# Attention product over whole rows with block-diagonal weights, in a fused attention and feed-forward layer

## The reference, cut to what matters

```python
q = layernorm(silu(causal_dwconv(h @ Wq, ...)))     # per head, 128 features
k = layernorm(silu(causal_dwconv(h @ Wk, ...)))
v = h @ Wv
beta = sigmoid(h @ Wb + bb);  gate = silu(h @ Wg)
def step(S, inp):                                   # over the 64 tokens
    q_t, k_t, v_t, b_t = inp
    S = (1.0 - b) * S + b * (v_t[..., :, None] * k_t[..., None, :])
    return S, einsum('bhvk,bhk->bhv', S, q_t)
x = x + (o * gate) @ Wo
# adapters, in the second part
xa = einsum('btd,brd->btr', x, A[idx]);  delta = einsum('btr,bor->bto', xa, Bm[idx]) * s[idx]
```

## Time and profile before

| | us |
|---|---|
| median of the 3 runs shown | 2570.62 (2568.57 to 2571.15) |
| the profiled execution | 2573.15 |
| its span, first to last instruction | 2571.4 |
| PE busy | 2450.2 (95%) |
| DVE busy | 1633.6 (64%) |
| ACT busy | 1072.2 (42%) |
| POOL busy | 783.9 (30%) |
| mean granted TensorE clock | 0.979 |

### The profile page before, as it was taken

The page is one execution under the profiler, slowest core; times in us unless marked ns, Lnnn a source line. Parts: engine busy times, 40 slices in busy tenths (PEclk is TensorE's granted clock), DMA queues, the critical chain, the costliest instruction groups (busy, mean ns, idle before and its releaser), DMA issues. The chain is left out here.

```text
span 2571.4 us, 38384 instructions
## 1 busy us (share of the span) xinstructions
PE 2450.2 (95%) x14292; PEld 1849.9 (72%) x14292; DVE 1633.6 (64%) x2653; ACT 1072.2 (42%) x1615; POOL 783.9 (30%) x636
## 2 busy tenths in 40 slices
PE   7789899999999999999999999999999999999976
PEld 5567677777777777777777777777777777777754
DVE  4666456676667756576566766667666775657653
ACT  4554444444435334443434434444443533444321
POOL 3465433322323222232233232232132322223230
PEclk9899999999999999999999999999999999999987
DMA  7786766567665776666676676656757577666750
GB/s 233 255 309 220 258 224 231 194 204 258 201 222 185 238 232 199 207 202 226 212 231 196 201 249 212 222 187 219 253 192 228 186 231 233 205 203 203 228 173 17
DMA packets 326962, 551.38 MB, mean 214 GB/s; under 512 B 98354, under 2 KB 122970, under 8 KB 326778
## 3 DMA queue, kind: packets, MB, share of 16 engines
q1 hardware_dynamic: 315778, 529.75, 62.2%
q10 hardware_dynamic: 11000, 19.18, 2.3%
HBM read 495.08 MB, written 53.74 MB: 213 GB/s over the span
## 5 line engine op out<-in xcount | busy, mean ns | idle before, releaser
L526 POOL TENSOR_TENSOR og_lo<-gt,og_hi 128x512 fp32r<-128x512 f32 x128 | 181.6, 1418 | 1128.3 <-ACT og_hi L1040 1128.3
L1110 PE MATMUL pj_a<-ht_hi,wq 128*128 128x512 f32 x1024 | 361.3, 414 | 30.8 <-ACT gt L1033 21.3
L1110 PE MATMUL pj_a<-ht_hi,wg 128*128 128x512 f32 x1024 | 355.5, 408 | 17.2 <-DMA wg<-parts_g 12.9
L812 DVE SCALAR_TENSOR_TENSOR y_q<-pj_a,conv,y_q 128x504 f32<-128x504 f32 (+2 forms) x384 | 281.1, 732 | 137.9 <-ACT y_q L1016 128.7
L1110 PE MATMUL pj_b<-ht_hi,wk 128*128 128x512 f32 x1024 | 346.7, 399 | 8.4 <-DMA wk<-parts_k 8.3
L1110 PE MATMUL ring<-wo,og_hi 128*128 128x512 f32 x1024 | 324.3, 398 | 5.2 <-issue 5.2
L1110 PE MATMUL ring<-wv,ht_hi 128*128 128x512 f32 x1024 | 320.5, 394 | 4.5 <-POOL wv L516 4.5
L812 DVE SCALAR_TENSOR_TENSOR y_k<-pj_b,conv,y_k 128x504 f32<-128x504 f32 (+2 forms) x384 | 281.4, 733 | 56.0 <-ACT y_k L1016 46.8
L522 POOL TENSOR_TENSOR y_k<-y_k,sq_k 128x512 f32<-128x512 f32 x128 | 170.8, 1335 | 462.2 <-DMA sq_k<-m_rows 462.1
L1110 PEld LDWEIGHTS pj_b<-ht_hi,wk 128*128 128x128 f32 x1024 | 192.4, 188 | 107.1 <-issue 52.0
L1110 PEld LDWEIGHTS pj_a<-ht_hi,wq 128*128 128x128 f32 x1024 | 197.6, 193 | 80.2 <-issue 24.9
(11 more groups left out here) (202 smaller groups left out, 4645.6 us busy)
## 6 DMA issues: line engine op xcount, KB each, us to landing
wq<-parts_q SPq DMA_DIRECT2D x112, 512.0 KB, 4.2
wk<-parts_k SPq DMA_DIRECT2D x112, 512.0 KB, 6.2
wg<-parts_g SPq DMA_DIRECT2D x112, 512.0 KB, 5.9
wv<-parts_v SPq DMA_DIRECT2D x112, 512.0 KB, 6.5
wo<-parts_o SPq DMA_DIRECT2D x112, 512.0 KB, 6.7
sq_q<-m_rows SPq DMA_DIRECT2D x110, 256.0 KB, 3.8
sq_k<-m_rows SPq DMA_DIRECT2D x110, 256.0 KB, 4.5
sq_q<-r_rows SPq DMA_DIRECT2D x110, 256.0 KB, 3.5
```

The source lines that it names most:

```text
L526: G.tensor_tensor(og_lo[:, u % OG_RING, :], gt[:, u % GT_RING, :], og_hi[:, u % OG_RING, :].bitcast(F32), ALU.subtract).then_inc(S["oglo"], 1)
L812: V.scalar_tensor_tensor(out=yy[:, :, k:], in0=pp[:, :, :L - k], scalar=conv[:, i, h, 3 - k:4 - k], in1=yy[:, :, k:], op0=ALU.mult, op1=AL ...
L1110: last = T.matmul(psum, a, b, start=start and n == 0 and m == 0, stop=stop and n == len(pairs) - 1 and m == 2)
```

## The change

1. **The product with v.** A new tile `decay_bd` of 128 x 512 is zeroed once by GpSimd. `weigh` writes the weighed scores of even sequences to its upper 64 rows and of odd ones to its lower 64 rows, each at its own 64 columns, in two instructions of 64 partitions x 256. Every 128 columns then hold two diagonal blocks and zeros beside them. `attend` makes four products, each with 128 rows of v as weights and 128 columns of `decay_bd`, all in the ring's bank; m0 is no longer written by it.
2. **The gate.** `gate_out` is one instruction of 128 x 512. The semaphore `og_odd` is gone: `score` and `scan` of the next unit wait for `weighed` instead of for the gate and the product; `weigh` waits for the preceding unit's product.
3. **The adapter product** is scaled in place in its PSUM bank, which is released after the low part is made; `xam` and two semaphores are gone, `gamma_cols` moves to `acc`, and `load_x(1)` also waits until it was sent off.

```diff
 def adapt(g, i):
-    V.tensor_tensor(rows8(xam[:]), rows8(ring_bank("xa", g, i)[:, 0:HALF]), sc.broadcast_to([P, HROWS, L]),
-                    ALU.mult).then_inc(taken_sem("xa", g, i), 1)
-    dve.wait_ge(*taken("xa", g, i))
+    down = ring_bank("xa", g, i)[:, 0:HALF]
+    V.tensor_tensor(rows8(down), rows8(down), sc.broadcast_to([P, HROWS, L]), ALU.mult).then_inc(S["xam_mul"], 1)
+    dve.wait_ge(S["xam_mul"], 2 * g + i + 1)
...
 def scan(u):
     if u:
-        dve.wait_ge(*made("pv", u - 1))
+        dve.wait_ge(S["weighed"], 2 * u)
...
 def weigh(u):
     dve.wait_ge(S["scores"], u + 1)
     dve.wait_ge(S["scanned"], u + 1)
-    V.tensor_tensor(decay[:], m0[:, 0:HALF], decay[:], ALU.mult).then_inc(S["weighed"], 1)
+    if u:
+        dve.wait_ge(*made("pv", u - 1))
+    else:
+        dve.wait_ge(S["setup_pool"], 9)
+    for b in range(2):
+        half = slice(b * L, (b + 1) * L)
+        V.tensor_tensor(even_odd(decay_bd[half, :], b), m0[half, 0:HALF].rearrange("p (i t) -> p i t", t=L),
+                        decay[half, :].rearrange("p (i t) -> p i t", t=L), ALU.mult).then_inc(S["weighed"], 1)
...
 def gate_out(u):
-    for b, bank_ in enumerate((ring_bank("pv", u, 0), m0)):
-        th = even_odd(t, b)
-        V.tensor_tensor(th, bank_[:, 0:HALF].rearrange("p (i t) -> p i t", t=L), th, ALU.mult
-                        ).then_inc((taken_sem("pv", u), S["og_odd"])[b], 1)
+    V.tensor_tensor(t, ring_bank("pv", u, 0)[:], t, ALU.mult).then_inc(taken_sem("pv", u), 1)
...
 def score(u):
     if u:
-        pe.wait_ge(S["og_odd"], u)
+        pe.wait_ge(S["weighed"], 2 * u)
...
 def attend(u):
-    pe.wait_ge(S["weighed"], u + 1)
+    pe.wait_ge(S["weighed"], 2 * u + 2)
...
-    for b in range(ROWS):
-        at, cols = L * (b % 2), slice(b // 2 * L, (b // 2 + 1) * L)
-        mm = T.matmul((ring_bank("pv", u, 0), m0)[b % 2][:, cols], v[at:at + L, s % 2, b // 2, j * P:(j + 1) * P],
-                      decay[at:at + L, cols], start=True, stop=True)
+    for i in range(HT):
+        cols = slice(i * P, (i + 1) * P)
+        mm = T.matmul(ring_bank("pv", u, 0)[:, cols], v[:, s % 2, i, j * P:(j + 1) * P], decay_bd[:, cols],
+                      start=True, stop=True)
```

More of the change, by code:

```diff
@@ L137, in adaln_attn_ffn @@
         decay = sb("decay", [P, HALF])
+        decay_bd = sb("decay_bd", [P, GROUP])
         gt = sb("gt", [P, GT_RING, GROUP])
@@ L149, in adaln_attn_ffn @@
         b_hi, b_lo = sb("b_hi", [P, D], F32R), sb("b_lo", [P, D], F32R)
-        xam = sb("xam", [P, HALF])
         xam_hi, xam_lo = sb("xam_hi", [P, HALF], F32R), sb("xam_lo", [P, HALF], F32R)
@@ L179, in adaln_attn_ffn @@
         conv_rows, small_rows = gt[0:H, 0:2, :], gt[0:H, 2, :]
-        gamma_cols = xam[0:KC, 0:P]
+        gamma_cols = acc[0:KC, 1, 0, 0:P]
         TAB_LOADS, LATE_LOADS = 4 + 4 + 1, 1 + 1 + 2
@@ L191, in adaln_attn_ffn @@
             sq_q sq_k seed newton_a newton_b rr n_q n_k aff_q aff_k
-            scanned og_odd oghi oglo ht_hi beta_done keep_done x2_hi xam_mul xam_hi xam_lo ssq absmax small
+            scanned oghi oglo ht_hi beta_done keep_done x2_hi xam_mul xam_hi ssq absmax small
             row_seed qa qb quant biased scaled""".split()
@@ L304, in load_x @@
                     sp.wait_ge(*made("sw", 0, KC - 1))
+                    sp.wait_ge(S["gamma_out"], 16)
                 elif g > 1:
@@ L509, in _ @@
                                pattern=[[RANK, NAD]], channel_multiplier=-1).then_inc(S["setup_pool"], 1)
+            pool.memset(decay_bd[:], 0.0).then_inc(S["setup_pool"], 1)
             def split_lo(block_):
@@ L700, in adapt @@
                 sc = ad_scale[:, b0:b0 + HROWS].rearrange("p (b o) -> p b o", o=1)
-                V.tensor_tensor(rows8(xam[:]), rows8(ring_bank("xa", g, i)[:, 0:HALF]), sc.broadcast_to([P, HROWS, L]),
-                                ALU.mult).then_inc(taken_sem("xa", g, i), 1)
-                dve.wait_ge(*taken("xa", g, i))
+                down = ring_bank("xa", g, i)[:, 0:HALF]
+                V.tensor_tensor(rows8(down), rows8(down), sc.broadcast_to([P, HROWS, L]), ALU.mult).then_inc(S["xam_mul"], 1)
+                dve.wait_ge(S["xam_mul"], 2 * g + i + 1)
                 if i:
                     dve.wait_ge(*made("h", g, 1))
-                V.tensor_copy(xam_hi[:], xam[:]).then_inc(S["xam_hi"], 1)
+                V.tensor_copy(xam_hi[:], down).then_inc(S["xam_hi"], 1)
                 dve.wait_ge(S["xam_hi"], 2 * g + i + 1)
-                V.tensor_tensor(xam_lo[:], xam[:], xam_hi[:].bitcast(F32), ALU.subtract).then_inc(S["xam_lo"], 1)
+                V.tensor_tensor(xam_lo[:], down, xam_hi[:].bitcast(F32), ALU.subtract).then_inc(taken_sem("xa", g, i), 1)
             def row_scales(g, p):
@@ L1036, in gated_hi @@
                 act.wait_ge(*taken("pv", u))
-                act.wait_ge(S["og_odd"], u + 1)
                 if u >= OG_RING:
@@ L1195, in dense @@
                         pe.wait_ge(S["wo_in"], wo_loads("h", g))
-                pe.wait_ge(S["xam_lo"], 2 * g + t // 2 + 1)
+                pe.wait_ge(*taken("xa", g, t // 2))
                 free_bank("h", g, t)
```

## The result

The changed kernel takes 2559.68 us (median of 9 runs, 2550.77 to 2563.38); the kernel before, timed on the same chip between them, 2571.92 (9 runs, 2568.57 to 2578.60). The ratio is 0.9949 [0.9936, 0.9962]; it is estimated from the single runs and is not quite the quotient of the two medians (0.9952). By the medians the change saves 12.2 us, where 28.2 were forecast. The profiled execution took 2562.26.

A forecast was written before the change was run, and what follows sets the result against it. TensorE's stream was taken as the bound between 410 and 2490 us. 37.1 + 1.0 - 2.4 - 4.1 - 2.0 - 0.7 - 0.7 = 28.2 us saved, from 2573.15 to 2544.9 profiled, 2542.4 as median; range 2532 to 2557.

The forecast's parts named there:

- The attend step: TensorE, last 512-column product to third q product: 1.93 us becomes 1.59, saving 0.34 per unit, mostly border gaps.
- How often it counts: The 0.34 us counts in 109 attend steps, units 15 to 123: 37.1 us; the 15 units before add 1 us.
- (a): Slot 10, g projection's wait for wg: one attend step's 0.34 us is lost in 7 groups, 2.4 us.
- where it is given back: Step listing recurring TensorE waits, ended by something started earlier, that absorb savings: 2.4, 4.1 and 2.0, plus 0.7 us.
- (b): Slot 15, k projection's wait for wk: two attend steps, 0.68 us, are lost in 6 groups, 4.1 us.
- (c): Slot 0, q projection's wait for ht_lo: slot 15's attend step, 0.34 us, is lost in 6 groups, 2.0 us.
- (d): Slot 12, gate read ahead of q: about 0.1 us late in 7 groups, 0.7 us.
- VectorE: Split weighing and merged gate: +0.27 us per unit, +0.45 without overlap; only slot 10 pays, 0.7 us taken.
- B: VectorE and the loads fall behind in slots 8 to 10 and 13 to 15: 14 us left, 2556; chance 0.10.
- D: Lengthened waits in slots 10 and 15 make the clock fall, 3.3 us each; with all 13, 2585; chance 0.03.
- C: The absorbing waits move with TensorE and the first part gains too: 42 us saved, 2528.5; chance 0.05.
- E: Whole-row weight loads on TensorE don't hide: +0.55 us per unit, 60 in 109, 2630 us; chance 0.02.

The follow-up runs named there:

- e13: The changed kernel run again without further edits, on one chip with later runs: 2555.47 us, ratio 0.9941 to the kernel before.
- e9: The changed kernel with the eight cond loads issued in slot 10 instead of slot 13: 2544.88 us, ratio 0.9883.
- e10: The kernel before with the eight cond loads issued in slot 10 instead of slot 13: 2565.82 us, ratio 0.9970.
- e11: The changed kernel with cond loads in slot 10 and the head's own loads ahead of those of Wv, Wo and W2: 2530.24 us, ratio 0.9833.
- e12: The kernel before with cond loads in slot 10 and the head's own loads ahead of those of Wv, Wo and W2: 2561.58 us, 0.9958.
- e2: The kernel before with only its weighing split into two instructions of 64 rows: 2576.01 us, ratio 1.0015.
- e3: The changed kernel with one weighing of 128 x 256 instead of two, block-diagonal layout left out (result not the reference's): 2554.7 us, ratio 0.9928.
- e16: The changed kernel with the product with v as eight of 64 columns over whole rows instead of four of 128: 2628.86 us, ratio 1.0214.
- e4: The changed kernel with five added 512-column products ahead of the waits in slots 15 (wk) and 10 (wg), groups 1 to 7: 2550.87 us, 0.9928.
- e14: The changed kernel with five added 512-column products ahead of the waits in slots 15 and 10, a repetition: 2551.44 us, ratio 0.9925.

## Why the prediction was wrong

**The attend step: right.** 1.59 us by the sum, 1.59 measured, in each of its three parts. The border gaps are gone, as argued. Whole slots shorten by 0.36, 0.02 more than I used.

**How often it counts: right but for slot 0.** That slot shortens by 0.13 instead of 0.36 in groups 2 to 6 and is 0.37 longer in group 1 (1.8 us given back in six groups). Its attend step follows four float32 transposes of 16 x 16 and not 512-column products. The gap ahead of the step is 0.14 in both kernels, and afterwards its second half starts 0.22 behind the first, where it is 0.11 elsewhere. I had read one border and used it for all; in slot 9, behind bf16 transposes, 0.27 is saved.

**(a) Slot 10: the mechanism right, the size low.** Forecast 2.4 for wg and 0.7 for VectorE in seven groups; 4.3 in six were measured in the profiled pair and 6.9 with the trace of e13. The gap for wg grew by 2.5 and 3.6, that for the weighing by 0.6 and nothing; one fall of the clock lies there in the first trace (2047.9) and three in the other, for which the sum had nothing.

**The step that failed: "where it is given back".** The sum let the wait for wk in slot 15 take 4.1 us, at full clock, and put the clock and every other load at nothing. (b), the wait itself: its anchor was right, its length was not fixed. The gap grew by 7.3 us in the profiled pair and by 3.4 with the trace of e13, so its size is met within what one execution scatters. With the cond loads elsewhere (e9, e10) the slot is 23.7 us in both kernels, and the difference between them goes from 14.2 to 20.9.

**The clock: put at nothing.** "The granted clock stays 1.00 between 410 and 2450 us" was wrong. Four falls lie in slots 10 and 15 of groups 1 to 6 in each of the two traces of the changed kernel, and none in that of the kernel before. By the mean clocks of all runs this is worth 5 us, and the added products took 4 to 8 us back.

**Other loads: put at nothing.** I named three waits and took the rest as covered. Slots 5 and 7 gave back 6.8 us, 5.7 with the trace of e13. Of the 6.8, 5.1 is the growth of their gaps ahead of the k projection (1.8 to 5.0 and 1.4 to 3.3), at loads that stand behind those of Wv, Wo and W2; with e13 it is 3.8. The busy share of 95% had hidden that these loads arrive with a few tenths to spare. With both edits (e11, e12), where no load ends these waits, the change is worth 31.3 us. That this is near 28.2 is partly luck. Without the terms for wg and wk the sum would be 28.2 + 2.4 + 4.1 = 34.7; in their place the waits for VectorE in slot 10 became longer than forecast (6.8 given back there in six groups).

**(c) and (d): right.** The wait in slot 0's q projection takes up the attend step of slot 15 (0.42 in the earlier trace rows; the gap there went from 0.69 to 0.84 although its border is gone). Slot 12 loses 0.13 a group, 0.1 forecast.

**VectorE: the mechanism named, the size too low.** +0.51 per unit instead of +0.27, above the bound of +0.45, for which 0.7 us was put in the sum. e2 and e3 give 1 to 5. Ahead of the attend steps of the other slots in groups 1 to 6 the weighing still ends 1 us or more early, as was said. Of the 3.7 us by which TensorE's wait for it grows in e2, 1.5 lie in slot 10 (four times), 0.9 in the first part and 1.4 in the tail; the 0.7 of the sum were for slot 10 alone.

**The rivals.** B was what happened in kind (14 us left by its count, 12.2 measured), but by the loads and the clock more than by VectorE, and with a chance of 0.10. That its number is so near is luck, since it has no term for the clock. D came in part: I wanted 9 of 13 waits to fall and priced one at 3.3 us. There were four in the one trace and five in the other, mostly of 3.4 us at half clock, which is 1.7 us each. What I held against it, that no wait of the steady part is longer than 2.73 us, gave no protection: a wait of 2.38 us (a gap of 2.77) had a fall behind it. C's premise, that absorbing waits move along, holds nowhere. E is excluded by 0.112 us per half, in the changed kernel itself and in e16.

**What is missing, summed.** From 28.2 to 12.2 are 16 us. Counted from the profiled pair: loads in slots 5, 7 and 15 beyond the forecast 5.1 + 3.2 = 8.3, the clock about 5 by the mean of the runs (7.1 in slots 10 and 15 of this pair), the weighing 1 to 4, slot 0 1.8. That is 16 to 19. In the repetition 10.1 us are missing (28.2 to 18.1), and the same count with its trace gives 3.8 - 0.7 = 3.1 for the loads and 11 to 14 in all. Something else may have gained a little (the start of group 1 is 1.7 us earlier, but it varies between 325.9 and 337.0 among kernels). The share of loads and of the clock can't be cut cleanly and stays open, since the falls stand behind the waits for loads: the added products of e4 and e14 took 4 to 8 us back, e9 14.2.

## What to carry to other kernels

An engine at 95% is bound by itself only up to the next thing that is nearly late: before a saving per step is multiplied by the steps, read for each load in the period how long ahead of its use it lands, and take the saving away from that margin. What stands in front of a needed load in an issue queue can count for more than the load (here 9.3 us of picked loads, against 6 to 8 us from the issue of wk to its use), and moving it can be worth as much as the saving: 14.2 us from one line in the changed kernel (7.5 in the kernel before), against 12 to 18 from the change. The longer waits of TensorE cost the clock behind them too, and matrix work of no use put into them seems to have won part of it back. And one trace is one execution: a wait that is read slot by slot should be read in a second one too, before its growth is put down to the change.

## What the runs showed of the hardware

- fp32 halves over whole rows are 0.11 us apart with 128 columns and with 64 (e16). Half-row halves come in pairs at the same 0.11, with 0.09 us more at the border in front and 0.19 behind; over whole rows the border in front is gone (0.23, kernel after and e16).
- Two VectorE multiplications of 64 rows on different partitions take 0.87 us together, and the next instruction starts 0.90 after the first; two of 128 rows on the same ones start 0.33 apart, for 0.40 of duration. Splitting one of 0.41 by rows costs 0.57.
- At a wait of TensorE of 2.82 or 3.85 us the granted clock went to half (1.2 GHz) for 3.4 and 6.8 us, behind the first and from the last 1.8 us of the second on; after one of 1.86 it stayed at 2.4 GHz. The length alone doesn't tell: a gap of 2.77 us between products had a fall behind it (slot 15 of group 4, kernel after), one of 2.95 (slot 10 of group 1, kernel before) had none.
- Eight DMA issues whose source is picked by value hold SyncE's queue for 9.3 to 9.7 us.
